# Two fp16 parts instead of three bf16 parts, and attention scores of two heads side by side in TensorE

## Chip, cores and metric

The kernel runs on one core of one Trainium2 chip. The metric is the device time of a run in microseconds, the median of several runs. Engines: PE (TensorE, matmuls), ACT (ScalarE), DVE (VectorE), POOL (GpSimd), SP (SyncE, which here only issues DMAs).

## The reference

One block of a gated cross-attention layer and one of a self-attention layer with a mixture of experts. Cut to what matters (`B, L, D = 4, 512, 256`, 16 heads of 16):

```
q = layernorm(x) @ wq.T + bq;  k, v = ctx @ wk.T + bk, ctx @ wv.T + bv
x = x + tanh(g_xattn) * (softmax(q k^T / 4) v)              # per batch and head, 512 x 512 scores
s = layernorm(x);  q, k = rope(s @ Wq), rope(s @ Wk_c @ Wk);  v = s @ Wv_c @ Wv
y = rmsnorm(s + (softmax(q k^T / 4) v) @ Wo)
x = x + tanh(g_ffn) * rmsnorm(y + shared_ffn(y) + top2_experts(y))
```

Everything is fp32 in the reference.

## The kernel before

The attention is done in eight instances `INST`: four cross (one for each batch), then four self. An instance has four groups of four heads (`NG`, `HG`), a group has 16 steps (`STEPS`), one for each unit: one head and one tile of 128 keys against 512 queries. So there are 512 units in 32 groups.

- **Parts.** q and k are split into three bf16 parts each (`NPART`), whose products of six terms (`NTERM`, `Q_PART`, `K_PART`) give the precision of fp32. The terms stand one above the other in 96 rows (`STK`). Part one is a copy by ACT (`first_part`, `part0`), `rest` a subtraction on POOL, part two a copy by ACT (`second_part`, `part1`), part three a subtraction on POOL (`third_part`, `part2`). SP writes the parts to DRAM and loads them back stacked, four DMAs for each group (`stack`).
- **Maxima.** `max_pair` makes the scores of one head with queries on the partitions, two tiles of queries into two banks, and DVE's `row_max` reduces both (L1136). Banks 2 to 5 are a ring of two such pairs. Eight maxima make a group; they run `LEAD` = 12 maxima ahead of the exps. DVE splits the 16 maxima of a group into two bf16 parts (`m2`), PE turns them (`turn_max`, after step `AT_MAX` = 9), ACT copies them to `mTs` and, at step `AT_ROWS` = 11, issues the DMA that puts them as two more rows (98, `KROWS`) below the stack of q. They stand against ones in k, so that the score matmul subtracts the maximum.
- **Units.** PE makes the scores of a unit (L1653) with keys on the partitions, ACT the exp into `prob` (L891, `scale=SC`), and after every fourth unit PE multiplies four heads with their values (`values`, L1629; fp32, each head with its 17 output rows in its own 32 columns of the array). `copy_values` copies a group's sum to `oT`, `turn_heads` turns it (L1617, in the ring), and DVE's `heads_out` divides.
- **Three banks.** Scores, turned maxima and all tiles of the projections of later instances take turns in `SCORE_BANKS` = 0, 1, 7; `take` waits until the slot three places back is empty.
- **Hooks.** `CROSS_STEPS`, `SELF_STEPS` and `FA_STEPS` say at which step relative to an instance the work for the next one (statistics, norm, tiles, parts) and for the output of the last is put into each engine's order. The engines run their orders strictly; the steps are written out by hand. A cross instance has ten tiles, a self instance nine, an output four. A tile is made by PE and emptied by ACT or DVE (`OWNER`).
- **After** the last group follow the feed-forward part, sorting and experts (from 538 us on), which the change leaves alone. SP's order is `stack(n)` for one instance after another.

Of the kernel before, what the change touches and what calls it, by code (L numbers as in the profile page):

```python
# [7 lines left out]
BF16 = mybir.dt.bfloat16  # L8
# [26 lines left out]
def flamingo_block(nc, x, ctx_in, g_xattn, g_ffn, wq, bq, wk, bk, wv, bv,  # L35
# [27 lines left out]
    SCR = [16 * 5, 16 * 3]  # L63
    SC = 1.0 / float(DH) ** 0.5
    VM = DH + 1
    MROWS = MPART * HG * TT
# [13 lines left out]


    HOOKS = {}

    def hook(n, step, *what):
# [3 lines left out]
    CROSS_STEPS = [("stats", 0, -34), ("norm", 1, -20), ("norm", 0, -16), ("tile", 2, -12), ("empty", 2, -12), ("tile", 0, -11),  # L88
        ("empty", 0, -11), ("tile", 3, -10), ("empty", 3, -10), ("tile", 1, -6), ("empty", 1, -6), ("tile", 4, -5),
        ("empty", 4, -5), ("tile", 5, -5), ("empty", 5, -5), ("tile", 6, -4), ("empty", 6, -4), ("part0", 0, -3),  # L90
        ("part1", 0, 1), ("rest", 0, 1), ("empty", 8, 2), ("tile", 8, 2), ("part2", 0, 2), ("tile", 7, 3),
        ("empty", 7, 3), ("part0", 1, 3), ("rest", 1, 4), ("tile", 9, 5), ("empty", 9, 5), ("part1", 1, 7),
        ("part2", 1, 10)]
    SELF_STEPS = [("stats", 0, -28), ("norm", 0, -21), ("norm", 1, -20), ("tile", 0, -14), ("empty", 0, -14), ("tile", 1, -9),
        ("empty", 1, -8), ("tile", 4, -4), ("empty", 2, -3), ("empty", 4, -3), ("tile", 2, -3), ("tile", 3, -2),
        ("empty", 3, -2), ("tile", 5, -1), ("empty", 5, 0), ("sum", 0, 1), ("tile", 6, 2), ("empty", 6, 2),
        ("sum", 1, 2), ("tile", 7, 5), ("empty", 7, 5), ("part0", 0, 5), ("rest", 0, 5), ("tile", 8, 7),
        ("empty", 8, 7), ("rest", 1, 8), ("part2", 1, 8), ("part0", 1, 10), ("part1", 0, 14), ("part2", 0, 14),
        ("part1", 1, 16)]
    FA_STEPS = [("fatile", 0, 12), ("faempty", 0, 12), ("faempty", 1, 15), ("fatile", 1, 15), ("faempty", 2, 19), ("fatile", 2, 19),  # L100
        ("fatile", 3, 23), ("faempty", 3, 23), ("fastats", 0, 32), ("nf", 0, 43)]

    SELF_NO = {m: sum(k_ == "s" for k_, _ in INST[:m + 1]) for m in range(NI)}
    for n in range(1, NI):
        m = n + 1
        if m < NI:
            for what, i, step in (CROSS_STEPS if INST[m][0] == "c" else SELF_STEPS):
                hook(n, step, what, m, i)
        if INST[n - 1][0] == "s":
            for what, i, step in FA_STEPS:  # L110
                hook(n, step, what, INST[n - 1][1], i)

# [12 lines left out]
    for u_ in range(NI * UNITS):  # L125
        n_, g_, s_ = u_ // UNITS, u_ // STEPS % NG, u_ % STEPS
        SLOTS.append(("unit", u_))
# [94 lines left out]
    with es:  # L222
# [23 lines left out]
        identb = sb("identb", [P, P], BF16)  # L246
# [26 lines left out]
        pp = mix[:, 0:NPART * 2 * L].bitcast(BF16).rearrange("p (x r o l) -> p x r o l", x=2, r=NPART, o=2)  # L273
# [6 lines left out]
        stacks = w2[:].rearrange("p k e d -> p (k e d)").bitcast(BF16).rearrange("p (x g h l) -> p x g h l", x=2, g=NG, h=HG)  # L280
        qs = stacks[0:KROWS, 0]
        ks = stacks[0:KROWS, 1]
        oT = sb("oT", [P, L], F32)
        negm = sb("negm", [P, 2, HG, TT], F32)

        m2 = sb("m2", [P, 2, P], BF16)
        mTs = sb("mTs", [MROWS, 2, P], BF16)
# [50 lines left out]

        scrq = nc.dram_tensor("scrq", [2, NTERM, DH * NH, L], BF16, kind="Internal").ap()
        scrk = nc.dram_tensor("scrk", [2, NPART, DH * NH, L], BF16, kind="Internal").ap()  # L340
# [22 lines left out]
        s_r0 = [sem(f"first_rest_ready{i}") for i in range(2)]  # L363
        s_p1 = [sem(f"second_part_ready{i}") for i in range(2)]
# [95 lines left out]
        def _(sp):  # L460
# [39 lines left out]
            def next_ctx(b):  # L500

                sp.wait_ge(s_ta, EMPTIED["proj", INST.index(("c", 0 if b == 2 else b - 1)), 3][1])
                load_ctx(b, ctxs[:])

            def stack(n):
                par = n % 2

                for g in range(NG):
                    ge(sp, s_stk[g], (n - 1) * 64)

                def put(X, part, ready):
                    sp.wait_ge(ready[X], n + 1)
                    p_ = parts[X][:, part]
                    if X or Q_PART.count(part) == 1:
                        d_ = (scrk[par, part] if X else scrq[par, Q_PART.index(part)]).rearrange("(o p) t -> p o t", p=P)
                        sp.dma_start(d_, p_).then_inc(s_scr[X], 16)
                        return
                    r = Q_PART.index(part)
                    c = Q_PART.count(part)
                    for o in range(2):  # L520
# [1320 lines left out]
```

## Time and profile before

| | us |
|---|---|
| median of 3 runs (789.3 to 790.07) | 789.88 |
| profiled run | 793.59 |
| its span | 791.8 |

| engine | busy us | share |
|---|---|---|
| PE | 746.5 | 94% |
| DVE | 512.4 | 65% |
| ACT | 408.1 | 52% |
| PE's weight loads | 342.7 | 43% |
| POOL | 225.6 | 28% |

Busy time is the union of an engine's instructions. Matmuls overlap in their pipeline: one alone takes some 0.38 us from start to end, but two that follow each other are shown as x2 with 0.60 us. So what counts is from start to start. In the timeline and the chain, a bracket at the end of a line gives the idle time before it and what ended it.

### The profile page before, as it was taken

To read this page: it belongs to the slowest core of one execution; us is meant where nothing else is said; L and a number is where in the kernel's file an instruction comes from. 1 tells how busy PE (TensorE), PEld (TensorE's weight loads), DVE (VectorE), ACT (ScalarE), POOL (GpSimd) and SP (SyncE) were. 2 spreads that over 40 slices of the span, in tenths; PEclk is the share of its full clock that TensorE was granted. 3 is DMA by queue.
4 is the path that set the end of the run, shared out by engine and by line. 5 is a ranking of instruction groups with operands and counts; after the bars stand their busy time and mean duration, and the time that the engine had idled before them with its cause. 6 is when DMAs were issued, how large, how long until landed. Compare 5 with 4: busy or idle time off the path is not lost.

```text
span 791.8 us, 10350 instructions
## 1 busy us (share of the span) xinstructions
PE 746.5 (94%) x3510; PEld 342.7 (43%) x3510; DVE 512.4 (65%) x777; ACT 408.1 (52%) x766; POOL 225.6 (28%) x342
## 2 busy tenths in 40 slices
PE   5889999999999999999999999999999999989994
PEld 3432343243233233233323423425645755458883
DVE  2588847956978878878797798743366022623764
ACT  2437867777767767876675777683211122222000
POOL 3360222314315405304222410010105622400654
PEclk9989999999999999999999999999999999999997
DMA  7792334216215414513411341006003734000010
GB/s 233 207 256 57 81 84 144 79 32 204 63 50 164 122 41 126 141 41 94 146 43 40 125 112 47 1 2 213 0 0 125 272 115 133 0 1 1 34 41 34
DMA packets 51892, 73.31 MB, mean 93 GB/s; under 512 B 7808, under 2 KB 42880, under 8 KB 51840
## 3 DMA queue, kind: packets, MB, share of 16 engines
q1 hardware_dynamic: 47248, 63.80, 27.4%
q0 software_dynamic: 2816, 8.46, 2.8%
q10 hardware_dynamic: 1776, 0.40, 0.3%
q8 instruction: 29, 0.48, 0.3%
q14 instruction: 23, 0.19, 0.1%
HBM read 45.04 MB, written 27.33 MB: 91 GB/s over the span
## 4 chain that ended last, share of the span: by engine, by line
PE 75%; DVE 14%; ACT 5%; issue 3%; DMA 1%; POOL 1%; ACTq 0%; DVEq 0%; POOLq 0%
PE ps L1483 35%; PE ps L1629 12%; PE ps L1653 11%; PE ps L1603 10%; DVE negm L1136 7%; ACT hS L891 3%; PE ps L1478 2%; DVE bst L1014 2%; PE ps L1617 1%; PE ps L1542 1%; DMA bv_bc<-in_L_xattn_bv_dram 1%; PE ps L1537 1%; PE ps L1563 0%; POOL out_dram L753 0%; DVE rows L1021 0%
## 5 line engine op out<-in xcount | busy, mean ns | idle before, releaser
L1136 DVE TENSOR_REDUCE negm<-ps 128x2 f32<-128x1024 f32 x256 | 304.0, 1221 | 75.8 <-PE ps L1603 68.0
L891 ACT ACTIVATE hS<-ps 128x512 f32<-128x512 f32 x512 | 280.6, 604 | 116.2 <-PE ps L1653 114.4
L1653 PE MATMUL ps<-w 98*128 98x512 bf16 x512 | 170.6, 386 | 4.8 <-DVE qk L1069 1.9
L1603 PE MATMUL ps<-w 96*128 96x512 bf16 x512 | 154.9, 383 | 7.3 <-DVE negm L1136 6.4
L1629 PE MATMUL ps<-hS,mix 128*17 128x512 f32 x1024 | 134.7, 598 | 0.2
L1653 PEld LDWEIGHTS ps<-w 98*128 98x128 bf16 x512 | 44.0, 97 | 157.0 <-ACT hS L891 76.7
L1603 PEld LDWEIGHTS ps<-w 96*128 96x128 bf16 x512 | 47.9, 99 | 59.7 <-DVE negm L1136 13.2
L1335 DVE SCALAR_TENSOR_TENSOR ctxs<-qk,ps 128x512 f32<-128x512 f32 x32 | 22.0, 688 | 76.3 <-ACT qk L925 51.1
L925 ACT ACTIVATE qk<-ps 128x512 f32<-128x512 f32 x32 | 19.1, 597 | 82.5 <-PE ps L1483 78.6
L1483 PE MATMUL ps<-w,hS 128*128 x256 | 55.7, 379 | 2.0 <-issue 2.0
L1483 PEld LDWEIGHTS ps<-w,hS 128*128 128x128 f32 x256 | 48.6, 190 | 9.4 <-issue 2.9
L615 POOL TENSOR_TENSOR mdif<-bst 128x4 f32<-128x4 f32 x12 | 2.5, 206 | 156.5 <-DVEq L976 156.5
L653 POOL TENSOR_SCALAR hS<-hS,tg 128x256 f32<-128x256 f32 x16 | 14.9, 931 | 99.6 <-DVEq L1162 99.6
L638 POOL TENSOR_TENSOR qk<-qk,mix 128x1024 f32<-128x1024 f32 x14 | 29.8, 2130 | 42.9 <-ACT mix L811 42.6
L633 POOL TENSOR_TENSOR qk<-qk,hT 128x1024 f32<-128x1024 f32 x8 | 18.8, 2350 | 76.1 <-DVEq L976 76.1
L1629 PEld LDWEIGHTS ps<-hS,mix 128*17 128x17 f32 x1024 | 17.0, 95 | 53.9 <-ACT hS L891 29.9
L643 POOL TENSOR_TENSOR mix<-qk,mix 128x1024 bf16<-128x1024 f32 x14 | 29.9, 2133 | 22.6 <-ACT mix L815 21.6
L1483 PE MATMUL ps<-fout,hS 128*128 128x256 f32 x128 | 30.6, 396 | 1.8 <-issue 1.8
L1483 PE MATMUL ps<-cT,fin 128*128 128x512 f32 x64 | 28.6, 595 | 0.7 <-ACT cT L918 0.7
L725 POOL DMA_INDIRECT scrf<-rows,place x16 | 15.7, 980 | 47.0 <-DVEq L976 42.4
L1338 DVE SCALAR_TENSOR_TENSOR hS<-ctxs,ps 128x512 f32<-128x512 f32 x32 | 22.0, 687 | 10.3 <-PE ps L1483 8.8
L1483 PEld LDWEIGHTS ps<-fout,hS 128*128 128x128 f32 x128 | 25.3, 199 | 7.3 <-issue 3.8
(210 smaller groups left out, 875.5 us busy)
## 6 DMA issues: line engine op xcount, KB each, us to landing
w<-scrq SPq DMA_DIRECT2D x32, 384.0 KB, 4.5
scrk<-mix SPq DMA_DIRECT2D x24, 256.0 KB, 2.1
scrq<-mix SPq DMA_DIRECT2D x16, 384.0 KB, 3.3
scrq<-mix SPq DMA_DIRECT2D x24, 256.0 KB, 2.5
w<-scrk SPq DMA_DIRECT2D x32, 192.0 KB, 2.9
w<-scrk SPq DMA_DIRECT2D x32, 128.0 KB, 2.9
w<-in_L_ffn_W_experts_dram SPq DMA_DIRECT2D x8, 512.0 KB, 8.0
mix<-scrf SPq DMA_DIRECT2D x4, 528.0 KB, 5.5
```

The costliest lines, as they stand in the source:

```text
L633: link(pool.tensor_tensor(qk[X][:], qk[X][:], rb[X], ALU.add))
L638: link(pool.tensor_tensor(qk[X][:], qk[X][:], parts[X][:, 0], ALU.subtract))
L643: link(pool.tensor_tensor(parts[X][:, 2], qk[X][:], parts[X][:, 1], ALU.subtract))
L891: nc.scalar.activation(prob[:, kt % PROB_SLOTS, s % HG, :], slot_bank(("unit", u)), ACT.Exp, scale=SC).then_inc(s_exp, 1)
L925: nc.scalar.activation(th[k % 4], end_full(f"{name}{b}", 2 * p), ACT.Tanh, scale=0.5).then_inc(s_th, 1)
L1136: V.tensor_reduce(negm[:, gi % 2, h, 2 * t2:2 * t2 + 2], ps[:, bank:bank + 2, :], AX.X, ALU.max, negate=True).then_inc(s_re, 1)
L1335: V.scalar_tensor_tensor(out=uu[:, k % 2, :], in0=th[k % 4], scalar=1.0, in1=end_full(f"{name}{b}", 2 * p), op0=ALU.add, op1=ALU.mult).the ...
L1338: V.scalar_tensor_tensor(out=hS[:, b * TT:(b + 1) * TT, p, :], in0=uu[:, k % 2, :].rearrange("p (t j) -> p t j", t=TT), scalar=0.5, in1=en ...
L1483: last = MM(o, w, r, start=(j == 0), stop=(j == len(terms) - 1))
L1603: last = MM(ps[:, bank + t, :], qs[0:STK, g, h, tt * P:(tt + 1) * P], ks[0:STK, g, h, :], start=True, stop=True)
L1629: last = MM(ps[32 * h:32 * h + VM, 6, :], vp[n % 2][:, kt, g * HG + h, :], prob[:, kk % PROB_SLOTS, h, :], start=(kt == 0), stop=(kt == TT ...
L1653: MM(take(("unit", u)), ks[:, g, h, kt * P:(kt + 1) * P], qs[:, g, h, :], start=True, stop=True).then_inc(s_sT, 1)
```

## The change

- q and k are first multiplied by a power of two ("fit") so that two fp16 parts hold them; the products need three terms, so a stack has 48 rows, and 50 with the two rows of the maxima (now divided by 32768, against 32768 in k).
- The powers come from the largest magnitude of contexts, weights and biases: DVE reduces them per partition (`magnitudes`), ACT's queue stores and reloads them across partitions, DVE computes powers, scaled biases and the scale of the exp (`powers`). Four such events: two at the start, two in the loop. The first part of k in the first instance waits for the first of them. The exp takes its scale from a tensor (`scale=esc[:, e:e+1]`).
- `second_part` and `third_part` are gone. What was `rest` now gives the second part.
- Stacks of two heads stand side by side in partitions 0 to 63 and 64 to 127 (`qs[j]`, `ks[j]`). `max_pair` takes one tile of queries of two heads instead of two tiles of one head. The scores come two units at once into two of the three banks, at even steps.
- `LEAD` 12 becomes 16, `AT_MAX` 9 becomes 11, `AT_ROWS` 11 becomes 15; the DMAs of the maximum rows (now two) go from ACT's queue to SP's, and SP's order follows the steps too (`put`, `get`, `max_rows`). All hook tables have other steps.
- ACT no longer waits for all biases before its first copy, and the value bias has a semaphore of its own. A tanh at the start loads ACT's table early.

```diff
-NTERM = 6
-NPART = 3
-Q_PART = [0, 0, 0, 1, 1, 2]
-K_PART = [0, 1, 2, 0, 1, 0]
-LEAD = 12
+NTERM = 3
+NPART = 2
+Q_PART = [0, 0, 1]
+K_PART = [0, 1, 0]
+HALF = 64
+MAX_ONE = 32768.0
+LEAD = 16
+PUT_LAG = 3
-AT_COPY, AT_HEADS, AT_MAX, AT_ROWS = 4, 8, 9, 11
+AT_COPY, AT_HEADS, AT_MAX, AT_ROWS = 3, 8, 11, 15
...
+    CROSS_STEPS = [("stats", 0, -38), ("mags", 0, -36), ("put", 0, -32), ("get", 0, -30), ("powers", 0, -26),
+        ("norm", 1, -20), ("norm", 0, -16), ("tile", 0, -11), ("empty", 0, -11), ("tile", 2, -11), ("empty", 2, -11),
+        ("tile", 3, -9), ("empty", 3, -9), ("tile", 1, -6), ("empty", 1, -6), ("tile", 4, -5), ("empty", 4, -5),
+        ("tile", 6, -3), ("empty", 6, -3), ("tile", 5, -1), ("empty", 5, -1), ("part0", 0, -1), ("empty", 8, 2),
+        ("tile", 8, 2), ("tile", 7, 3), ("empty", 7, 3), ("rest", 0, 4), ("tile", 9, 5), ("empty", 9, 5),
+        ("part0", 1, 5), ("rest", 1, 6)]
+    SELF_STEPS = [("stats", 0, -28), ("norm", 0, -22), ("norm", 1, -18), ("tile", 0, -15), ("empty", 0, -15),
+        ("tile", 1, -8), ("empty", 1, -7), ("tile", 4, -4), ("empty", 4, -3), ("empty", 2, -2), ("tile", 2, -2),
+        ("tile", 5, 0), ("empty", 5, 0), ("tile", 3, 1), ("empty", 3, 2), ("sum", 0, 3), ("empty", 6, 5), ("tile", 6, 5),
+        ("sum", 1, 6), ("part0", 0, 7), ("rest", 0, 7), ("empty", 7, 8), ("tile", 7, 8), ("tile", 8, 9), ("empty", 8, 9),
+        ("part0", 1, 14), ("rest", 1, 18)]
...
+        qs = [stacks[HALF * j:HALF * j + KROWS, 0] for j in range(2)]
+        ks = [stacks[HALF * j:HALF * j + KROWS, 1] for j in range(2)]
...
+            def max_rows(gi):
+                sp.wait_ge(s_mts, gi + 1)
+                n_ = MPART * HP * TT
+                for j in range(2):
+                    sp.dma_start(qs[j][STK:KROWS, gi % NG, :, :], mTs[j * n_:(j + 1) * n_, gi % 2, :]).then_inc(s_mrow, 16)
...
+            def put_magnitudes(e):
+                c, n_ = EVENTS[e]
+                act.wait_ge(s_mag, e + 1)
+                act.dma_start(scra[e], am[:, c:c + n_], allow_slow_non_contiguous=True).then_inc(s_mst, 16)
+
+            def get_magnitudes(e):
+                n_ = EVENTS[e][1]
+                act.wait_ge(s_mst, 16 * (e + 1))
+                ge(act, s_fit, e)
+                act.dma_start(amall[:, 0:P * n_], scra[e].rearrange("p n -> (p n)").unsqueeze(0).to_broadcast([P, P * n_])).then_inc(s_mld, 16)
...
                         nc.scalar.activation(prob[:, kt % PROB_SLOTS, s % HG, :], slot_bank(("unit", u)),
-                                             ACT.Exp, scale=SC).then_inc(s_exp, 1)
+                                             ACT.Exp, scale=esc[:, e:e + 1]).then_inc(s_exp, 1)
...
-                h, t2 = p // 2, p % 2
+                hp, tt = divmod(p, TT)
...
-                for t in range(2):
-                    tt = 2 * t2 + t
-                    last = MM(ps[:, bank + t, :], qs[0:STK, g, h, tt * P:(tt + 1) * P], ks[0:STK, g, h, :],
+                for j in range(2):
+                    last = MM(ps[:, bank + j, :], qs[j][0:STK, g, hp, tt * P:(tt + 1) * P], ks[j][0:STK, g, hp, :],
                               start=True, stop=True)
...
-                            pe.wait_ge(s_mrow, (gi + 1) * 16)
-                        MM(take(("unit", u)), ks[:, g, h, kt * P:(kt + 1) * P], qs[:, g, h, :],
-                           start=True, stop=True).then_inc(s_sT, 1)
+                            pe.wait_ge(s_mrow, (gi + 1) * 16 * 2)
+                        if s % 2 == 0:
+                            banks = [take(("unit", u + j)) for j in range(2)]
+                            for j in range(2):
+                                MM(banks[j], ks[j][:, g, h // 2, kt * P:(kt + 1) * P], qs[j][:, g, h // 2, :],
+                                   start=True, stop=True).then_inc(s_sT, 1)
```

## Rows read from the trace of the kernel before

**Rows 1.** Stretches: stretch, length, busy us of each engine, PE's clock, DMA.

```profile
114.10:176.90 62.80, 61.42 (x326) 22.14 (x325) 44.92 (x57) 46.57 (x89) 17.93 (x23) 1.00 0.33 98
239.80:300.60 60.80, 59.47 (x308) 19.28 (x308) 50.06 (x61) 44.64 (x85) 22.63 (x24) 1.00 0.37 108
```

**Rows 2.** Timeline of PE, one quad: start, length, engine, line, tiles, count.

```profile
215.87 0.61 PE L1653 MATMUL ps<-w 98*128 98x512 bf16 x2
216.31 0.60 PE L1603 MATMUL ps<-w 96*128 96x512 bf16 x2
...
217.71 1.05 PE L1629 MATMUL ps<-hS,mix 128*17 128x512 f32 x8
218.69 0.60 PE L1653 MATMUL ps<-w 98*128 98x512 bf16 x2
```

**Rows 3.** Timeline at the loop's end, where there are no maxima.

```profile
523.49 0.82 PE L1653 MATMUL ps<-w 98*128 98x512 bf16 x3
523.92 2.06 ACT L891 ACTIVATE hS<-ps 128x512 f32<-128x512 f32 x4 [0.68 <-PE ps L1653]
...
524.57 0.39 PE L1653 MATMUL ps<-w 98*128 98x512 bf16 x1 [0.26 <-ACT hS L891]
...
525.88 0.82 PE L1653 MATMUL ps<-w 98*128 98x512 bf16 x3
...
537.51 0.66 PE L1617 MATMUL ps<-identf,oT 128*128 128x128 f32 x4 [0.72 <-ACT oT L779]
```

**Rows 4.** Timeline of PE at a turn of heads.

```profile
260.52 0.60 PE L1617 MATMUL ps<-identf,oT 128*128 128x128 f32 x4
260.95 0.38 PE L1653 MATMUL ps<-w 98*128 98x512 bf16 x1
```

**Rows 5.** Timeline of DVE, maxima without a wait between them.

```profile
516.52 3.49 DVE L1136 TENSOR_REDUCE negm<-ps 128x2 f32<-128x1024 f32 x3
```

**Rows 6.** Timeline of PE at a full tile and at one with 64 rows.

```profile
233.73 1.88 PE L1483 MATMUL ps<-nT,fq 128*128 128x512 f32 x4
235.45 0.38 PE L1653 MATMUL ps<-w 98*128 98x512 bf16 x1
...
239.76 0.39 PE L1653 MATMUL ps<-w 98*128 98x512 bf16 x1 [0.49 <-DVE qk L1069]
240.08 1.12 PE L1537 MATMUL ps<-cT,fkv 64*128 64x512 f32 x2
241.13 0.39 PE L1653 MATMUL ps<-w 98*128 98x512 bf16 x1
```

**Rows 7.** Groups of ACT's instructions: count, busy us, mean ns, idle before.

```profile
L891 ACT ACTIVATE hS<-ps 128x512 f32<-128x512 f32 x512 | 280.6, 604 | 116.2 <-PE ps L1653 114.4
L779 ACT ACTIVATE oT<-ps 128x512 f32<-128x512 f32 x32 | 19.2, 600 | 1.2 <-PE ps L1629 1.2
...
L815 ACT ACTIVATE mix<-qk 128x1024 bf16<-128x1024 f32 x14 | 14.9, 1065 | 1.6 <-POOLq L639 0.8 <-ACT mTs L784 0.8
...
L825 ACT ACTIVATE qk<-ps,bqk 128x512 f32<-128x512 f32 x12 | 8.2, 687 | 19.4 <-PE ps L1483 17.0 <-PE ps L1563 2.5
```

**Rows 8.** Timeline of the start: first part, maximum, maximum rows, first score.

```profile
16.32 0.69 ACT L846 ACTIVATE mix<-ps,bqk 128x512 bf16<-128x512 f32 x1 [1.92 <-PE ps L1483]
...
37.89 1.23 DVE L1136 TENSOR_REDUCE negm<-ps 128x2 f32<-128x1024 f32 x1 [7.54 <-PE ps L1603]
...
50.11 0.73 ACTq L789 DMA_DIRECT2D w<-mTs  x1
...
52.44 0.37 SPq L516 DMA_DIRECT2D scrk<-mix  x1
...
52.53 0.61 PE L1603 MATMUL ps<-w 96*128 96x512 bf16 x1 [2.38 <-DVE negm L1136]
...
54.49 1.06 PE L1653 MATMUL ps<-w 98*128 98x512 bf16 x2
```

**Rows 9.** The chain that ended last, in order: start, length, what.

```profile
4.05 7.28 DMA bv_bc<-in_L_xattn_bv_dram
```

More of the change, by code:

```diff
@@ L94, in flamingo_block @@
[L94 to L99, printed above, removed]
@@ L106, in flamingo_block @@
         if m < NI:
+            last = 0
             for what, i, step in (CROSS_STEPS if INST[m][0] == "c" else SELF_STEPS):
                 hook(n, step, what, m, i)
+                if what in ("part0", "rest"):
+                    hook(n, step + PUT_LAG, "put_first" if what == "part0" else "put_rest", m, i)
+                    last = max(last, step + PUT_LAG)
+            STACK_AT[m] = last + 1
         if INST[n - 1][0] == "s":
@@ L111, in flamingo_block @@
                 hook(n, step, what, INST[n - 1][1], i)
+    for n in range(NI - 1):
+        for g in range(NG):
+            hook(n, max((g + 1) * STEPS, STACK_AT[n + 1]) + 1, "stack", n + 1, g)
+    hook(1, 4, "next", 3, 0)
+    for i in range(N_LATE):
+        hook(i + 1, 6, "late", 0, i)
     BEGIN = [2, 3, 6, 7, 0, 1, 4, 5, 8, 9]
@@ new lines, in put @@
+                    ge(sp, s_stk[g], (n - 1) * STACKED)
+                sp.wait_ge(s_spl[X] if part else s_p0[X], n + 1)
+                p_ = parts[X][:, part]
+                scr, terms = (scrk, K_PART) if X else (scrq, Q_PART)
+                at = [r for r in range(NTERM) if terms[r] == part]
+                if len(at) == 1:
+                    sp.dma_start(scr[n % 2, at[0]].rearrange("(o p) t -> p o t", p=P), p_).then_inc(s_scr[X], 16)
+                    return
+                r0, dr = at[0], at[1] - at[0]
@@ L558, in _ @@
             assert len(late) == N_LATE
-            stack(0)
+            sp.wait_ge(s_one, 1)
+            for X in (1, 0):
+                for part in range(NPART):
+                    put(0, X, part)
+            for g in range(NG):
+                get(0, 1, g)
+                get(0, 0, g)
             next_ctx(2)
@@ L824, in cross_tile @@
                         ge(act, s_spl[X], m)
-                    nc.scalar.activation(qk[X][:, o, :], full(key), ACT.Identity, bias=bqk[:, X, o:o + 1]).then_inc(s_ta, 1)
+                    act.wait_ge(s_fit, AT_EVENT[INST[m]] + 1)
+                    b = INST[m][1]
+                    f = 1 + b if X else 0
+                    nc.scalar.activation(qk[X][:, o, :], full(key), ACT.Identity, bias=bfit[:, f, o:o + 1],
+                                         scale=fit[:, f:f + 1]).then_inc(s_ta, 1)
             def self_tile(m, t):
@@ L1106, in empty @@
+                ready(s_spl[X])
             def empty(m, t):
@@ L1196, in _ @@
                                 stats(m)
+                            elif what == "mags":
+                                magnitudes(AT_EVENT[INST[m]])
+                            elif what == "powers":
+                                powers(AT_EVENT[INST[m]])
                             elif what == "empty" and OWNER[INST[m][0]][i] == "V":
@@ L1608, in turn_max @@
                 pe.wait_ge(s_m2, gi + 1)
-                o = take(("turned", gi))[:, 0:P // 2].bitcast(BF16)
-                last = TR(o, m2[:, gi % 2, :], identb[:])
+                o = take(("turned", gi))[:, 0:P // 2].bitcast(F16)
+                last = TR(o, m2[:, gi % 2, :], identh[:])
                 last.then_inc(s_mtf, 1)
```

345 lines of the change are left out of this document (187 added, 158 removed).

## The prediction

> **What bounds the kernel now.** The page first: PE is busy 94% of the span, DVE 65%, ACT 52%. I then read the groups by line, for what repeats, and the stretches, for one period of the attention loop (64 units of scores) for either kind of instance. In both stretches PE is at 98%, DVE at 72 to 82%, ACT at 73 to 74% [rows 1]. The last view is PE's timeline, because a busy PE may still be waiting inside its pipeline. There the loop is a fixed pattern, which I call a quad: four score matmuls, four maximum matmuls, four value products. There [rows 2] give 218.69-215.87 = 2.82 us per quad: eight matmuls at 0.2175 (two from 215.87 to 216.31; 1.74), 0.98 for the value products (217.71 to 218.69), and 0.10 left for the step into them. So PE's stream is the bound, in the stages 54.49 to 537.5 (483 us; first score and last turn of heads, [rows 3, 8]). The other 309 us aren't touched but for the start. A period sums to its work plus stalls: 122 quads at 2.82 and 6 at 2.39 (without maxima, [rows 3]) are 358; turned heads 32 x 0.44 [rows 4]; turned maxima 32 x 0.10; tiles 1.72 for a product (235.45-233.73, [rows 6]), about 0.44 for a transpose (as for heads), 1.05 for a small one (241.13-240.08): ten tiles of a cross instance 12.1, nine of a self instance 10.2, four of an output 4.3, together 78. Sum 453. So 30 of the 483 us are stalls.
>
> **The score and maximum matmuls.** Two heads with 50 (or 48) rows each go to partitions 0 and 64 and to two banks. If both stream at once, a pair takes 0.22 instead of 0.435. No row shows matmuls side by side in the rows of the array. The nearest are the value products: four heads in four column groups, fp32, x8 records in 1.05 [rows 2], where one after the other would be 8 x 0.2175 = 1.74; so side by side works there in full. Bounds 0.22 and 0.435; I take 0.22, being nearest to that row. PE's own work per quad falls to 4 x 0.2175 + 1.08 = 1.95, 0.87 less; that is 122 x 0.87 = 106 us if nothing else were late.
> The Trainium skill (TensorE: Matmul & The Clock Gate, section on packing small matmuls) says that row groups overlap too, with starts some 4 ns apart; by it the same 0.22 stands. No row here shows it.
>
> **What is late next: the exchange with ACT.** Before, a unit takes the next of three banks, so a score waits for the exp three units back. Now a pair takes two of three, and waits until the first exp of the pair before it is done. The tail without maxima shows the links: score start to exp start 0.43 (523.49 to 523.92), exp end to next score 0.05 (524.52 to 524.57) [rows 3]. The exp gets its scale from a tensor instead of a constant. The nearest row is the Identity with a bias from a tensor, 687 ns against 600 for the copy of the same size and 604 for the exp [rows 7]: bounds 0.60 and 0.69, I take 0.69, as that row has the operand. x4 in 2.06 gives 0.487 from exp to exp now, so 0.575 then, still under PE's pace.
> From the first pair of a quad to the second: 0.43+0.69+0.05 = 1.17, PE working 0.44 of it. From the second pair to the next quad: pair and maxima 0.44, step 0.10, values 0.98 = 1.52. A quad is 2.69, not 1.95: a gain of 0.13, with 0.73 of idle PE in the first half where a small piece can hide. At 0.60 per exp it would be 2.60. In the tail 1.17+1.30 = 2.47. All: 120 x 2.69 + 8 x 2.47 = 343, 15 less than 358.
> The Trainium skill (ScalarE: Activation LUTs, section on what an ACTIVATE and a table load cost) gives 93 ns for each pointer operand; the trace's 87 agrees, and by 93 the quad is 0.01 longer. It is the rule that speaks against this change.
>
> **Drains.** A 64-row product between full ones starts 0.32 after a matmul that needs 0.22, and ends after 1.05 where 0.86 would do: 0.30 for in and out [rows 6]. A full tile among full ones pays none: its 1.72 are four times 0.43. After the change the scores are 64-row and all full tiles pay 0.30; the 64-row tiles of k and v save it. Turned heads (0.44+0.30) mostly hide in the idle half: 0.4 each, 13 in all. Turned maxima 0.25: 8. A tile also takes a slot of the three banks, so the pair behind it waits for both exps (1.17 becomes 1.74). By the hooks: cross tiles 12.4 x 2, self tiles 8.9 x 4 (three of them in the idle half), outputs 4.3 x 3: 73. Together 94 against 95 before: nothing gained.
>
> **ACT.** The second parts (two copies of 1.065 per instance, [rows 7]) go; they were off the path. But ACT now has only 2.69-2.31 = 0.38 to spare in a quad. A norm (two at 0.49) costs 0.6 twice, a first part (1.05) about 0.8 once: 2 us for each of six instances, 12. Copies to oT 32 x 0.1 = 3. The maximum rows move to SP and to step 15, behind its puts and gets. Issue to landing was 2.3 (50.11 to 52.44, [rows 8]); from the turn at step 11 to the next group are 0.25+1.17+1.52 = 2.9, the chain needs about 3.1: 0.2 x 31 = 6. Exp, score and value product of the next group are behind that wait. SP's stacks are loaded 9 or more units before use, and carry half the bytes: zero, worth up to 1 us a stage if the cover went.
>
> **DVE.** A maximum is 1.221 long and 1.14 apart (3.49 for x3, [rows 5]): 2.27 in a quad of 2.69. Its lumps (statistics, rotations, heads) catch PE through the two-slot ring. I take 1.5 per instance, 9, and 3 for magnitudes and powers of two instances (for each a reduction of 1024 elements like a maximum, 1.2, and some 14 tiny ones with their waits; estimate 3.5, half of it in DVE's spare time; at most 4 each). The smaller splits on POOL are off the path.
>
> **The loop after:** 343+94+12+3+6+12 = 470, against 483: -13.
>
> **The start.** LEAD 16 instead of 12 puts four more maxima ahead of the first exp: 4 x 1.14 = +4.6. The magnitudes add reduction, store, load and powers before the first part of k, which began at 16.32 [rows 8]. A load landed after 7.28 there [rows 9]; I take 4 each way. Against that, ACT no longer waits for the value bias before copying cT, the third part is gone, and the stacks have half the bytes. First maximum 37.89 before, 37 to 44 after, I take 38.5: +0.6. POOL's memset lies beside the loads. Net +5.2.
>
> **Sum.** -13+5 = -8. The profiled run took 793.59 (span 791.80, 1.8 around it), the runs have the median 789.88, 3.7 under it. So 785.6 for a profiled one, and 789.9-8 = 782 as the median.
>
> **Rivals.**
> 1. The lumps overlap better than I add them, since each engine has 10 to 20% to spare. PE's load is 128 x 1.95+94 = 344, so the time is set by DVE (358 in the loop now, less overlap, some 366 after) and the exchange. If the drains hide too and stalls are 30 as now, the loop is 343+78+30 = 451: 789.9-32+5 = 763. For it: the idle 0.73 in every quad. Against it: one pair of lookahead. Chance 0.25.
> 2. Slower: a pair of banks leaves ACT no cushion, so its lumps go straight to PE. They are 11 to 12.6 per instance (8 copies at 0.49, norms 2.0, parts 2.1, oT 2.0, maxima 0.7). I count 12 of some 72 us; if half count, the loop is 494 and the time 789.9+11+5 = 806. It decides from 20 of the 72 on (then the loop has saved less than the start costs). For it: quads are at 2.69 with ACT at 2.31. Chance 0.3.
> 3. The pairs don't run side by side: the second half of a quad is 0.44 longer, 128 x 0.44 = 56: 838. Against it the value products. Chance 0.05.
> 4. The clock: with less work PE may be granted less. At 54.49 two matmuls took 1.06 instead of 0.61, after a wait of 2.38 on DVE in the lead [rows 8, 2]. With 16 maxima of 0.22 in 1.14 that lasts longer; a quad then costs 1.7 more, for 4 us of loop 2 to 3. In the range.
>
> **Chances.** Forecast (770 to 794) 0.4, rival 1 0.25, rival 2 0.3, rival 3 0.05. 0.2% (1.6 us) is about what a measurement can tell from no change. Of the forecast's 0.4, 0.24 lies under 788.3, 0.09 within, 0.07 above. Faster 0.5, same 0.1, slower 0.4 with the others. The range takes 754 to 810; the forecast's own is 770 to 794.
>
> **What would show it.** Right: PE's timeline with a pair in 0.22 and about 1.17 from the first to the second pair of a quad; the exp at 0.69; PE busy 85% in the loop, waits of the score load on the exp in most units. Wrong: quads under 2.5 (exchange mis-sized), first exp later than 61 or earlier than 56, waits on the maximum rows or stacks over 1 us per group, pairs at 0.43.

## The result and the profile after

The changed kernel takes 828.95 us (median of 4 runs, 824.61 to 833.34); the kernel before took 789.59 beside it. The ratio is 1.050, 95% interval 1.043 to 1.058: slower by 39 us, where 782 was forecast. Profiled were a run of 832.15 after and one of 793.59 before.

The page after: busy time, and PE and its granted clock in 40 slices of 20.8 us.

```profile
span 830.4 us, 10656 instructions
...
PE 690.9 (83%) x3510; PEld 302.5 (36%) x3510; DVE 523.8 (63%) x827; ACT 449.7 (54%) x753; POOL 192.3 (23%) x327
...
PE   5586788858878978878887888887999999999994
...
PEclk9795989989999999999999997998999999999998
```

The stretch from the first score to the last turn of heads, first the one of before, then the one of after (columns as in [rows 1]).

```profile
54.49:537.51 483.02, 469.76 (x2476) 160.11 (x2474) 374.07 (x471) 348.10 (x665) 125.67 (x212) 1.00 0.30 88
```

```profile
71.33:579.41 508.08, 411.74 (x2470) 120.98 (x2466) 373.24 (x493) 390.51 (x653) 96.54 (x145) 0.94 0.16 50
```

PE's busy time in the loop fell from 469.8 to 411.7, yet the loop took 25.1 more, and in it the granted clock fell from a mean of 1.00 to one of 0.94. There are two levels, 1.0 (2.4 GHz) and 0.5 (1.2 GHz), so that is 0.06/0.5 x 508 = 61 us at the lower one. The first score came 16.8 later. What follows the loop took 251.0 in place of 254.3.

The timeline of two quads after, PE and ACT (answering [rows 2, 3]).

```profile
84.39 0.39 PE L1753 MATMUL ps<-w 50*128 50x512 f16 x2 [0.65 <-ACT hS L943]
84.61 0.40 PE L1701 MATMUL ps<-w 48*128 48x512 f16 x2
84.93 1.05 PE L1727 MATMUL ps<-hS,mix 128*17 128x512 f32 x8
85.92 0.39 PE L1753 MATMUL ps<-w 50*128 50x512 f16 x2
86.14 0.38 PE L1701 MATMUL ps<-w 48*128 48x512 f16 x2
86.34 2.51 ACT L943 ACTIVATE hS<-ps,esc 128x512 f32<-128x512 f32 x4 [0.27 <-PE ps L1753]
87.17 0.39 PE L1753 MATMUL ps<-w 50*128 50x512 f16 x2 [0.65 <-ACT hS L943]
```

A pair is 0.39 long and the next matmul starts 0.22 after it: the two run side by side. From the first pair of a quad to the second are 87.17-85.92 = 1.25, from the second to the next quad 85.92-84.39 = 1.53: a quad of 2.78, against 2.82 before. PE stands 0.65 in it for the exp.

This is the shortest form. The next quad has the copy to `oT` ahead of its exps:

```profile
88.70 0.39 PE L1753 MATMUL ps<-w 50*128 50x512 f16 x2
88.83 0.60 ACT L819 ACTIVATE oT<-ps 128x512 f32<-128x512 f32 x1
...
90.15 0.39 PE L1753 MATMUL ps<-w 50*128 50x512 f16 x2 [0.85 <-ACT hS L943]
...
91.68 0.39 PE L1753 MATMUL ps<-w 50*128 50x512 f16 x2
```

PE stands 0.85 and the quad takes 2.98. Over all quads at the full clock that hold nothing but their four scores, four maxima and value products (counted by the starts of the matmuls in the two traces), before has 54 with a median of 2.82 and a mean of 2.91, after has 47 with 2.98 and 3.03. So the quads, which were to become 0.13 shorter, became longer on average.

The start (answering [rows 8, 9]): the chain of waits, and the timeline of ACT and DVE.

```profile
9.51 5.95 DMA scra<-am
15.49 4.20 DMA w<-scra
...
32.88 8.52 DMA scra<-am
41.42 5.05 DMA w<-scra
...
170.76 7.56 DMA scra<-am
178.34 4.59 DMA w<-scra
```

```profile
22.71 1.45 ACT L894 ACTIVATE mix<-ps,bfit,fit 128x512 f16<-128x512 f32 x2 [5.75 <-DVEq L1028]
...
41.80 0.60 ACT L864 ACTIVATE cT<-ps 128x512 f32<-128x512 f32 x1 [4.43 <-DMA scra<-am]
...
46.50 0.29 DVE L1095 TENSOR_REDUCE amx<-w 128x1 f32<-128x128 f32 x1 [9.42 <-DMA w<-scra]
...
49.91 1.23 DVE L1230 TENSOR_REDUCE negm<-ps 128x2 f32<-128x1024 f32 x1 [1.99 <-PE ps L1701]
```

The first part of k came at 22.71 in place of 16.32, and the first maximum at 49.91 in place of 37.89: the second event's load stands in DVE's order ahead of the maxima. The second of the two events inside the loop, on ACT and PE:

```profile
178.72 0.69 ACT L943 ACTIVATE hS<-ps,esc 128x512 f32<-128x512 f32 x1 [5.79 <-DMA scra<-am]
...
180.62 0.61 PE L1753 MATMUL ps<-w 50*128 50x512 f16 x2 [5.78 <-ACT hS L943]
...
181.58 1.91 PE L1727 MATMUL ps<-hS,mix 128*17 128x512 f32 x8
```

ACT's next exp stands behind the wait for its own store, PE behind ACT, and afterwards the value products take 1.91 where they take 1.05 at the full clock. The first event in the loop (store at 99.78) goes another way: its store landed after 1.4 and its load after 3.1, and there PE stood for a maximum, because DVE's search for magnitudes stood ahead of it:

```profile
101.22 0.61 PE L1701 MATMUL ps<-w 48*128 48x512 f16 x2 [2.00 <-DVE negm L1230]
```

From 100 us on the clock is at the lower level for some 10 us there too.

### The profile page after: what moved, and what is told of

It is laid out like the page before. It is cut to its first block, busy times and chain, and to the rows that moved or that the text cites. A ratio compares the mean times of both kernels' runs of the same rounds, so it can differ in the third digit from the quotient of the medians.

```text
span 830.4 us, 10656 instructions
## 1 busy us (share of the span) xinstructions
PE 690.9 (83%) x3510; PEld 302.5 (36%) x3510; DVE 523.8 (63%) x827; ACT 449.7 (54%) x753; POOL 192.3 (23%) x327
## 4 chain that ended last, share of the span: by engine, by line
PE 51%; DVE 17%; ACT 15%; issue 7%; DMA 6%; POOL 2%; ACTq 0%; DVEq 0%; POOLq 0%
PE ps L1582 30%; ACT hS L943 11%; DVE negm L1230 9%; PE ps L1727 8%; PE ps L1753 6%; PE ps L1701 3%; DMA scra<-am 3%; POOL scrf L762 2%; PE ps L1715 2%; DMA w<-scra 2%; PE ps L1577 1%; DVE bst L1133 1%; ACT rows L845 1%; DVE qk L1177 1%; DMA bqk<-in_L_xattn_bq_dram 1%
## 5 line engine op out<-in xcount | busy, mean ns | idle before, releaser
L943 ACT ACTIVATE hS<-ps,esc 128x512 f32<-128x512 f32 x512 | 323.4, 684 | 85.4 <-PE ps L1753 77.2
L1753 PE MATMUL ps<-w 50*128 50x512 f16 x512 | 105.1, 402 | 76.6 <-ACT hS L943 67.7
L1727 PE MATMUL ps<-hS,mix 128*17 128x512 f32 x1024 | 144.9, 640 | 0.4 <-ACT hS L943 0.4
L1701 PE MATMUL ps<-w 48*128 48x512 f16 x512 | 108.4, 403 | 18.2 <-DVE negm L1230 15.6
L1753 PEld LDWEIGHTS ps<-w 50*128 50x128 f16 x512 | 28.5, 93 | 215.6 <-ACT hS L943 125.4
L685 POOL TENSOR_TENSOR mix<-qk,mix 128x1024 f16<-128x1024 f32 x14 | 30.0, 2142 | 76.6 <-ACT mix L859 75.9
L1701 PEld LDWEIGHTS ps<-w 48*128 48x128 f16 x512 | 27.0, 95 | 52.1 <-DVE negm L1230 22.6
L1250 DVE RECIPROCAL rec<-ps 128x16 f32<-128x16 f32 x32 | 8.1, 254 | 35.8 <-PE ps L1715 35.8
L1582 PE MATMUL ps<-rope_sb,fin 128*128 128x512 f32 x64 | 28.2, 593 | 0.0
L1582 PE MATMUL ps<-wT,fin 128*128 128x512 f32 x64 | 28.1, 592 | 0.0
```

What stands on the lines that cost most here:

```text
L685: link(pool.tensor_tensor(parts[X][:, 1], qk[X][:], parts[X][:, 0], ALU.subtract))
L943: nc.scalar.activation(prob[:, kt % PROB_SLOTS, s % HG, :], slot_bank(("unit", u)), ACT.Exp, scale=esc[:, e:e + 1]).then_inc(s_exp, 1)
L1582: last = MM(o, w, r, start=(j == 0), stop=(j == len(terms) - 1))
L1701: last = MM(ps[:, bank + j, :], qs[j][0:STK, g, hp, tt * P:(tt + 1) * P], ks[j][0:STK, g, hp, :], start=True, stop=True)
L1727: last = MM(ps[32 * h:32 * h + VM, 6, :], vp[n % 2][:, kt, g * HG + h, :], prob[:, kk % PROB_SLOTS, h, :], start=(kt == 0), stop=(kt == TT ...
L1753: MM(banks[j], ks[j][:, g, h // 2, kt * P:(kt + 1) * P], qs[j][:, g, h // 2, :], start=True, stop=True).then_inc(s_sT, 1)
```

## The experiments

Where nothing else is said a time is a median, and the kernel before took 788.5 to 789.3 beside each set of runs. "Profiled" is the time of the run whose trace was kept. "Start" is the time of its first score, "loop" the stretch from there to its last turn of heads. The profiled run can lie some us to either side of the median, so starts and loops are compared with that in mind. Ratios are to the kernel before.

| kernel | us | ratio, 95% interval | profiled | start | loop | clock in span |
|---|---|---|---|---|---|---|
| before | 789.6 |  | 793.6 | 54.49 | 483.0 | 0.986 |
| after | 828.95 | 1.043 to 1.058 | 832.2 | 71.33 | 508.1 | 0.949 |
| e1_const | 794.72 | 1.004 to 1.010 | 799.0 | 50.97 | 494.0 | 0.962 |
| e2_const_single | 798.04 | 1.007 to 1.013 | 799.0 | 52.60 | 492.3 | 0.968 |
| e3_const_serial | 910.16 | 1.134 to 1.155 | 911.3 | 54.00 | 603.1 | 0.876 |
| e4_late_get | 813.83 | 1.029 to 1.035 | 813.6 | 70.19 | 491.0 | 0.962 |
| e5_const_imm | 783.18 | 0.991 to 0.996 | 779.2 | 51.21 | 473.8 | 0.981 |
| e6_const_early | 810.31 | 1.026 to 1.031 | 807.8 | 51.30 | 502.1 | 0.958 |
| e7_const_warm | 798.74 | 1.010 to 1.017 | 799.3 | 56.26 | 490.5 | 0.973 |
| e8_pe_mags | 812.40 | 1.026 to 1.033 | 814.3 | 56.35 | 501.9 | 0.959 |
| e9_before_ptr | 801.45 | 1.013 to 1.020 | 797.9 | 50.52 | 495.0 | 0.991 |
| e10_pe_mags2 | 810.36 | 1.024 to 1.033 | 806.4 | 53.98 | 496.4 | 0.966 |
| e11_const_imm_lead12 | 777.53 | 0.981 to 0.989 | 780.5 | 47.21 | 480.8 | 0.970 |
| e12_const_imm_single | 780.07 | 0.985 to 0.992 | 780.2 | 52.09 | 475.6 | 0.981 |
| e13_before_short | 862.66 |  | 869.1 | 55.99 | 558.8 | 0.902 |
| e14_own_mags | 799.49 | 1.011 to 1.020 | 798.6 | 53.34 | 493.0 | 0.972 |
| e15_pe_mags2_lead12 | 802.99 | 1.009 to 1.019 | 804.3 | 50.21 | 498.2 | 0.971 |

**The whole search for magnitudes taken out** (e1). Constant powers of two stand in `fit`, `bfit` and `esc`; the scale of the exp is still a tensor.

```diff
-        ("mags", 0, -36), ("put", 0, -32), ("get", 0, -30), ("powers", 0, -26),
+            for f, v in enumerate(FITS):
+                mark(V.memset(fit[:, f:f + 1], v))
```

> The changed kernel without the search for magnitudes: the powers of two, the scaled biases and the scale of the exp are constants set at the start, so no reductions of magnitudes, no store and reload across partitions, no waits for them; everything else stays, the exp still reads its scale from a tensor. Theory A (the four magnitude events, with the waits of ACT and DVE in order and the lower clock behind them, carry most of the loss): the first score comes at about 57 instead of 71.3 us, the groups around 100 and 175 us lose their 5 and 10 us, and the time is 829-31 = 798. Rival B (the exchange of score banks with ACT carries it): the events cost no more than the 5 us forecast for them, and the time stays at 818 or more.

Measured 794.72, 34 under after. The search was costed at 3 + 0.6 us in the sum; it is the larger part of the loss, 20 us of it ahead of the first score (71.33-50.97) and 14 in the loop.

**Only the reload later** (e4). It is the changed kernel with `("get", 0, -22)` and `("powers", 0, -14)` in place of -30 and -26.

> The changed kernel with the reload of the magnitudes moved from 2 to 10 steps behind their store in ACT's order (and the powers from step -26 to -14); only for the two events in the loop. Theory A: ACT no longer stands 5.8 us and 1.4 us before the reload, and PE's clock does not fall there: 10 to 14 us less, about 817. Rival: what ACT waited for was hidden by PE, and the time is within 3 us of 829.

Measured 813.83, 15 less, all of it in the loop (508.1 to 491.0). So the loop's share of the loss comes with where store, reload and powers stand in the orders, and the search's own work is not needed to explain it.

**What of the search costs** (e14, e8, e10, e15). In e14 every instruction of the search stays and only the way across the partitions is left out:

```diff
-                dve.wait_ge(s_mld, 16 * (e + 1))
-                link(V.tensor_reduce(amx[:, c:c + n_], amall[...], AX.X, ALU.max))
+                for i in range(c, c + n_):
+                    mark(V.memset(amx[:, i:i + 1], LARGEST[i]))
```

> The changed kernel with its search and the arithmetic of the powers on DVE at their steps, but the largest magnitudes set to fixed values in place of the store, the load and the reduction across partitions, which it leaves out. Theory A, the crossing costs the most: e1_const (795) plus DVE's own 3 to 6 us: 797 to 802. Rival B, DVE's instructions in the order of the maxima cost most of it: 806 to 812.

Measured 799.49: the search's own work costs 799.5-794.7 = 5 (an uncertain figure, since e1's ten runs spread from 789.9 to 800.3), the crossing 829.0-799.5 = 29. The first maximum stands at 31.89 there, 18.0 before the 49.91 of after, and the first score also 18.0 before (53.34 against 71.33): the start's loss is the crossing, one for one.

e8 crosses by a matmul, `MM(bank, am[:, c:c + 1].to_broadcast([P, P]), identf)`, whose 128 columns hold the values of all partitions on every partition; no DMA is left.

> The changed kernel with its search for magnitudes whole, but each column of magnitudes brought to all partitions by one matmul against the identity in a bank of the scores, in place of the store to DRAM and the load back. Theory A, the events cost by their two transfers and by the engines that stand behind them: e1_const (795) plus the search's own work on DVE (3 to 5 us): 798 to 801, first score near 57 us. Rival B, the search's instructions and its order on DVE cost most of it: 810 or more.

Measured 812.40, as rival B had it. The start is 15 better than after's, but the loop only 6, where e14's is 15 better. PE's timeline tells why:

```profile
87.66 2.05 PE L1570 MATMUL ps<-identf,am 128*128 128x128 f32 x8 [4.45 <-DVEq L1012]
...
89.75 0.69 DVE L1080 TENSOR_REDUCE amx<-ps 128x4 f32<-128x512 f32 x1 [2.29 <-PE ps L1570]
...
90.18 1.91 PE L1729 MATMUL ps<-hS,mix 128*17 128x512 f32 x8
```

I had put PE's matmul at the same step as DVE's search. PE stood 4.45 for DVE, then DVE 2.29 for PE, and the clock fell: again engines that stand in order for each other. e10 sets search, matmul and arithmetic apart by 5 steps and one.

> e8_pe_mags (812) with the steps of an event apart: the search of the weights at step -41, that of the context at -38, the matmuls at -33 and the arithmetic at -32, so that PE and DVE no longer stand for each other (PE stood 4.45 us for the search, DVE 2.29 for the matmuls, and the clock fell behind them). Theory A, an event costs by the engine that stands in order for another: 802 to 806, group 3 of 19.7 us going to 14 to 15. Rival B, by its own instructions on DVE (4.5 us in event 2), which keep the maxima's banks from PE wherever they stand: 809 to 813.

Measured 810.36 (806.39 to 812.78), inside rival B's range, so setting the steps apart bought 2 us at most. The profiled run, the fastest of the four, has its loop 5.5 shorter than e8's. What the median still loses against e1 was not taken apart further: it can be DVE's own instructions, as the rival says, or the clock, which in the two slower runs is 0.953 and 0.954 and in the fastest 0.966. e15 is that kernel with `LEAD` 12, and computes all that the changed kernel does.

> e10_pe_mags2 (810, profiled span 804.6) with twelve pairs ahead of the loop in place of sixteen; nothing of the computation is left out. Theory A, -5 as e11_const_imm_lead12 against e5_const_imm: 801 to 806, still over before. Rival B, DVE's search and not the lead sets the first score: 808 to 812.

Measured 802.99, within the expected range: 26 better than the changed kernel, 14 worse than the one before.

**The exp's scale as an immediate** (e5, e9). e5 is e1 with `scale=SC / (...)`, a number.

> Leaves the search for magnitudes out (constant powers of two, as in e1_const) and gives the exponential its scale as an immediate again. In e1_const three exps in a row take 1.93 us (0.58 each beyond the first), before 1.57 (0.49), and PE stands 0.65 us in each quad for them. Theory A, the exchange of two banks for two exps sets the quad now: one pair of each quad waits, two exps less 0.087 each, so -0.17 x 128 = -22 from e1_const's 795: 773 (768 to 782), quads of 2.85 going to 2.68. Rival B, the quad is set by the matmuls and their drains and the wait is only shifted: 790 to 795, ACT idle grows by what the exps give back.

Measured 783.18, 11.5 less than e1. It is Theory A's side, but half its size: 22 were expected, and 783.2 is outside its 768 to 782. The shortest of its quads:

```profile
203.44 0.39 PE L1756 MATMUL ps<-w 50*128 50x512 f16 x2
...
203.87 2.23 ACT L939 ACTIVATE hS<-ps 128x512 f32<-128x512 f32 x4 [0.63 <-PE ps L1756]
204.60 0.39 PE L1756 MATMUL ps<-w 50*128 50x512 f16 x2 [0.56 <-ACT hS L939]
...
206.13 0.39 PE L1756 MATMUL ps<-w 50*128 50x512 f16 x2
```

From first pair to second it is now 1.16, to the next quad 1.53: 2.69, against 2.78. One exp of each quad lies in the chain, not two: 0.09 x 128 = 11.5. Some of the difference of the medians is the clock's: e1's three runs with a clock of 0.977 took 789.9 to 791.9, e5's three with 0.974 and 0.975 took 782.4 to 784.2, some 8 apart. The other way round, the kernel before with a scale from a tile:

> The kernel before, its exponential given the same scale from a tile in place of an immediate. Theory A, the 0.09 us that each exp takes longer is hidden where PE sets the quad (2.82 us, against four exps in a row of 4 x 0.58 = 2.31): 789 to 792. Rival B, it costs wherever it stands, as e1_const against e5_const_imm (12 us): 799 to 803.

Measured 801.45, so the rival was right and PE's cover did not exist. The clock is no part of it (0.991 in the span, 0.986 before). A quad of the kernel before, with the load of the fourth score's weights (PEld):

```profile
128.12 0.60 PE L1653 MATMUL ps<-w 98*128 98x512 bf16 x2
...
128.55 2.06 ACT L891 ACTIVATE hS<-ps 128x512 f32<-128x512 f32 x4 [1.02 <-PE ps L1653]
...
129.00 0.59 PE L1653 MATMUL ps<-w 98*128 98x512 bf16 x2
129.19 0.10 PEld L1653 LDWEIGHTS ps<-w 98*128 98x128 bf16 x1 [0.32 <-ACT hS L891]
```

The same place in e9, and the starts of the next two quads:

```profile
128.95 0.61 PE L1658 MATMUL ps<-w 98*128 98x512 bf16 x2
...
129.38 2.42 ACT L895 ACTIVATE hS<-ps,esc 128x512 f32<-128x512 f32 x4 [0.49 <-PE ps L1658]
...
129.83 0.68 PE L1658 MATMUL ps<-w 98*128 98x512 bf16 x2
...
130.12 0.10 PEld L1658 LDWEIGHTS ps<-w 98*128 98x128 bf16 x1 [0.41 <-ACT hS L895]
...
131.86 0.60 PE L1658 MATMUL ps<-w 98*128 98x512 bf16 x2
...
134.77 0.39 PE L1658 MATMUL ps<-w 98*128 98x512 bf16 x1
```

Quads of 2.91 in place of 2.82: again 0.09 x 128 = 11.5, and the loop grew by 12.0. So two ways lead from a quad's first score to its fourth. On PE it is five matmuls: 5 x 0.2175 = 1.09. Through ACT the fourth score needs the bank of the first: 0.43 to its exp, 0.60 for the exp, 0.04 to the load of the weights (129.19-128.55-0.60), and some 0.03 to the matmul, 1.10 in all. In the kernel before the two ended together, beside a PE that was busy throughout. With the longer exp the load comes at 130.12-128.95 = 1.17 in place of 129.19-128.12 = 1.07, and the two last scores show 0.68 in place of 0.59: the fourth waits. So this link was a second bound of the same length from the start, and pairs that stream in half the time could shorten only what stands behind it. In the changed kernel that part fell from 1.73 to 1.53, and the link itself grew from 1.10 to 1.25.

**Scores side by side** (e2, e12, e3). e2 and e12 give each unit its own step and bank again:

```diff
-                            banks = [take(("unit", u + j)) for j in range(2)]
-                            for j in range(2):
-                                MM(banks[j], ...)
+                        MM(take(("unit", u)), ks[h % 2][...], qs[h % 2][...], ...)
```

> As the kernel without magnitudes, and in addition each unit takes its own bank and is multiplied at its own step again, as before the change; two heads still stand one above the other, maxima are still made in pairs. This undoes only that a pair of scores takes two of three banks. If the exchange with ACT sets the quad (2.78 us in the changed kernel), a score now waits for the exp three units back and a quad falls to about 2.45 (PE: six slots of 0.2175, 0.10, 0.98 = 2.39; ACT 4 x 0.575 = 2.31): 0.3 x 128 = 38 us less than the kernel without magnitudes, some 5 to 10 of it given back by DVE, about 768. If PE's drains and the tiles set it, the time is that of the kernel without magnitudes or 128 x 0.2 more, since the scores no longer run side by side.

> e5_const_imm (783) with the scores' matmuls one bank and one step each again (each still 50 rows high, the maxima still side by side); leaves the search for magnitudes out. Theory A, with the immediate PE sets the quad, and each single score pays its own streaming and drain as in the kernel before: quads from 2.68 back to 2.8, 128 x 0.13 = +17 at most, 790 to 797. Rival B, ACT and the exchange set it, as e1_const and e2_const_single were alike: 781 to 786.

Measured 798.04 against e1's 794.72 and 780.07 against e5's 783.18. The first is 30 over the 768 of its main case and in the range of its other one (no change, or up to 26 more); the second is 1 under the rival's range. The differences have opposite signs and are about as large as the spread of the runs. Taking two banks at a time for the scores of two heads is worth 3 us at most in either direction. In e3 both matmuls of a pair use the same 64 rows, so that they must follow each other; the odd heads of its output come from the even heads' stacks.

> As the kernel without magnitudes, but both matmuls of every pair, scores and maxima, read the stacks of partitions 0 to 63, so both stand in the same rows of the array and can't run side by side; the scores of the odd heads are therefore those of their neighbours. The order of the instructions and all waits are the same. If side by side works as the timeline shows (two in 0.39), the second half of each quad is 0.44 longer, 128 x 0.44 = 56 us more than the kernel without magnitudes; if PE has that much to spare behind ACT and DVE, under 20.

Measured 910.16 (896.07 to 912.06), 115 over e1, and 101 in its fastest run. As expected, the pairs do run side by side in e1; the size is twice the 56. Groups of e3 at the full clock take 13.46 where those of e1 take 11.9 to 12.1 (the time between two turned maxima): 1.4 x 32 = 45 for the streaming. The other 70 go with the clock: groups of 22.8 stand there with the clock at 0.50, and from 100 to 140 us PE is busy 40.00 of 40.00 at that level. This was the first sign of what e13 tells below.

**The maximum rows earlier** (e6): `AT_MAX, AT_ROWS = 5, 8` in place of 11, 15, as sixteen pairs of lead allow.

> Leaves the search for magnitudes out, as e1_const; the turned maxima are taken at step 5 of a group in place of 11 and their rows loaded at step 8 in place of 15. Theory A: the rows of maxima end their load after the scores of the next group are due (14 waits of about 1 us, 13.5 us in the profile of after): these go, -8 to -13 from 795: 782 to 787. Rival B: the waits hid the exchange with ACT, which is late next: 792 to 796.

Measured 810.31, 16 worse where 8 to 13 better were expected. By the turns of heads the profiled loop is 8.1 longer: nothing in the self instances (a period of 60.0 for 60.2), 2.1 in one group of the cross instances, 2.3 in the last two full groups, the rest in small. So in the self instances the rows' load was no bound. The move also puts other work of ACT and SP at other steps, so in the cross instances it can't be told from that. Why it is slower, and what the median has beyond the profiled loop, stays open.

**PE kept busy ahead of the loop** (e7): 144 small matmuls in the lead.

> Leaves the search for magnitudes out, as e1_const, and adds 16 + 16 x 8 small fp16 matmuls on PE between the maxima ahead of the loop, into a bank not yet in use, so that PE does not stand idle there. Theory A, the fall of the clock ahead of the loop costs 5 to 8 us (granted clock 0.5 from 43 to 68 us in e1_const, group 1 of 20.4 us): clock stays at 1.0 over 45 to 68 us, the group falls to about 14 to 16, 787 to 790 in all. Rival B, DVE's maxima and the row load set that stretch at either clock: 794 to 797.

Measured 798.74, 4 worse. The clock held to 1.00 in most of the lead, the first score came 5.3 later, and the clock fell at 60 us all the same. It bought nothing; but since the added matmuls also put off the first score, it does not tell what a lead at the full clock alone would give.

**The lead** (e11): `LEAD` 12 in e5.

> e5_const_imm (783) with twelve pairs of maxima ahead of the loop in place of sixteen; leaves the search for magnitudes out. Theory A, each of the four maxima stands ahead of the first score with 1.15 us: -4.6, 778 to 779. Rival B, another wait ends last there (the rows' load, the parts of the second instance): 782 to 784.

Measured 777.53, -5.7 (-4.6 expected), with the start 4.0 earlier. It leaves the search out, so it is no substitute for either kernel.

**What the clock follows** (e13). The kernel before, its matmuls of maxima and scores 48 rows high:

```diff
-                    last = MM(ps[:, bank + t, :], qs[0:STK, g, h, ...], ks[0:STK, g, h, :],
+                    last = MM(ps[:, bank + t, :], qs[0:48, g, h, ...], ks[0:48, g, h, :],
-                        MM(take(("unit", u)), ks[:, g, h, ...], qs[:, g, h, :],
+                        MM(take(("unit", u)), ks[0:48, g, h, ...], qs[0:48, g, h, :],
```

> The kernel before with the matmuls of maxima and scores 48 rows high in place of 96 and 98, the same columns and order; leaves out the three smaller of the six products of parts and the maxima's two rows. Theory A, low matmuls let the granted clock fall, busy PE or not (e3_const_serial: over 200 us at 0.50 with 94% busy): falls inside the loop, clock under 0.975, 797 to 830. Rival B, the falls follow PE's waits: clock as before (0.986), 787 to 791.

The products left out are the last three terms; by `Q_PART` and `K_PART` one of them (q's second part with k's first) is no smaller than one that stays, which changes nothing in the timing. Measured 862.66, above both ranges: 73 us longer (before: 789.33 beside it) with half the rows in these matmuls, and still 52 longer in the fastest run. Stretches of before, then of e13, on PE alone (start and end, length, PE busy, clock, DMA):

```profile
80.00:100.00 20.00, 18.96 (x113) 1.00 0.29 77
100.00:150.00 50.00, 48.91 (x256) 1.00 0.36 106
```

```profile
80.00:100.00 20.00, 20.00 (x64) 0.50 0.14 34
100.00:150.00 50.00, 50.00 (x166) 0.62 0.08 23
150.00:200.00 50.00, 49.11 (x262) 1.00 0.40 118
```

The same instructions in the same order were granted 1.00 in every such stretch of before. Both kernels enter the loop at the lower level, after PE stood 2.3 us for a maximum in the lead; before is back at the full clock within 5 us, e13, with PE never standing, stays at the lower level from 60 to 135 us. Later it falls again, with PE busy 98.55 of 100 us from 200 to 300 (clock 0.88; before 97.82 at 1.00). The loop's mean is 0.86. The four runs say the same: 841.17, 856.21, 869.12 and 869.82 us at mean clocks of 0.938, 0.916, 0.902 and 0.900.

What this does in the changed kernel is not shown. In e13 and e3 some 50 rows work at a time; in after, e1 and e5 two stacks of 50 do, side by side, and e5's loop has a mean clock of 0.99. And the falls in after come where PE had been standing: the one at 178.8 us within the wait of 5.78, the one near 510 us after this:

```profile
505.00:510.00 5.00, 3.26 (x25) 0.99 0.18 52
```

So for after PE's waits are the cause at hand. That is argued; no run tells the two apart there.

The Trainium skill (TensorE: Matmul & The Clock Gate, section on why this matters for your kernels) asks for a busy TensorE without idle gaps. e13 was busy for all of 80 to 100 us at 0.50, so here that was not enough; the measurement decides.

## Why the prediction was wrong

The forecast was 782, the time 829: 47 to explain. The experiments add up to the time: 783 with an immediate scale and no search (e5), the tensor scale +11.5 (e1), the search's instructions +5 (e14), the crossing +29 (after). The forecast had the same terms: 3+0.6 for the search, 120 x 0.087 = 10.4 for the tensor scale, so 768 for what e5 is. Of the 47, then, 30 are the search (34 in place of 3.6), 15 the rest of the change (783 in place of 768), 1 the scale.

**The start, +16.8 for +5.2.** LEAD's four maxima were right (4.6 forecast; 4.8 is what the stretch from first maximum to first score grew, and 4.0 the start between e5 and e11). The step that failed is "+0.6" for the first maximum: it counts one event, "before the first part of k". The second one, for the second context, stands in DVE's order just ahead of the first maximum (9.42 of idle). "I take 4 each way" was short too: the ways took 5.95 and 4.20, and in the second event 8.52 and 5.05; but the first part of k came only 6.4 later. The first maximum was forecast for 38.5, within 37 to 44, and came at 49.91, 12.0 later than before. Without the crossings it came at 31.89 (e14), so all else in the start was faster than I took it to be. "First exp later than 61" was named as a sign of being wrong, and it came.

**The search in the loop.** It was costed as 3 us on DVE, with nothing for the queue. The instruction that starts the reload waits on ACT for the store (7.56), and the next exp is queued behind it: 5.79 of idle on ACT, 5.78 on PE, in the second event of the loop. This was in the diff; I did not ask what stands behind a DMA's wait on the engine that issues it. With the wait moved (e4) the loop is as short as without any search (491.0 and 494.0).

**Side by side.** Right: 0.22 for a pair, as forecast; the third rival did not happen. The working that led there had a slip: 8 x 0.2175 = 1.74 is the pace of the bf16 matmuls, while an fp32 record takes 0.43 (1.72 for the four of a full tile, [rows 6]). One after the other the value products would take 8 x 0.43 = 3.44, so 0.98 shows side by side even more clearly; the conclusion stands.

**The quad.** 2.69 forecast, 2.78 measured at best, and for an immediate 2.60 and 2.69. The mechanism was right (first to second pair by way of ACT, then PE's 1.52) and one link was short: exp end to next score was taken as 0.05 from [rows 3]; here it is 87.17-86.34-0.68 = 0.15, in e5 204.60-203.87-0.60 = 0.13. What makes the difference was not tried. About 0.09 x 120 = 11 us. The copies to oT were taken at 0.1 for each of 32 groups; where a quad holds nothing else the copy costs 0.20 (2.98 in place of 2.78), so by an estimate from that row 6 us in place of 3. These 14 are most of e5's 15.

**PE as the only bound.** "PE's stream is the bound" was half of the truth: e9 shows that from first to fourth score a second way of the same length lies beside it. I had its links in [rows 3] and used them for after, but never for before, where 0.43+0.60+0.05 = 1.08 against PE's 5 x 0.2175 = 1.09 would have shown it.

**The clock.** Rival 4 gave it 2 to 3 us, only at the start. In the loop it was at the lower level for some 60 us after, 40 in e1 (0.04/0.5 x 494), and before only in the first 5 us. What a fall costs: the group of turned maxima that ends near 522 in after takes 16.57, the same one in e4 at the full clock 13.07. The two stretches:

```profile
510.00:520.00 10.00, 9.12 (x42) 0.50 0.05 16
```

```profile
500.00:510.00 10.00, 8.22 (x61) 1.00 0.14 41
```

So 3.5 us for about 10 at the lower level, and for 61 an estimate of 20 us. It is part of the crossing's 29 and of e1's distance to the forecast, not on top of them. That the clock would fall inside the loop, where waits of PE now stand, is what no step of mine had; whether the lower matmuls add to it (e13) stays open for this kernel.

**Rivals.** The second (806) had the right side and the right place in ACT, but by lumps of copies; these did cost in the instances with cross tiles (groups of 25.0 to 26.4 in e1 where before had 23.9) and not in the self instances (a period of 60.2 for 60.9). Drains and maximum rows were not measured one by one. e1's loop is 494 against 467 forecast without the search; the quad's link explains 11 of the 27, the copies to oT 3 and the clock's 40 us some 13, the last two by estimates. That the rest cancels can be luck.

## What to carry to other kernels

Where an engine is busy 98% of the time, ask in the kernel before what every other way between the same two instructions would take. Here it was 1.10 us against 1.09: faster matmuls gave nothing on that stretch, and 0.09 us more on the other way cost 12 us at once. A wait for a DMA belongs on an engine with nothing queued behind it; the same bytes cost 15 us less when only the steps between store, reload and powers grew. Work taken out of TensorE can be paid for in its clock, by the waits that appear (after) or by rows that are no longer used (e13), so read the granted clock of the loop before and after.

## What the runs showed of the hardware that was not expected

- TensorE, 97% busy in the loop with matmuls 96 and 98 rows high, was granted 1.00 in it but for the first 5 us; with the same matmuls 48 rows high it stood at the lower level for about 156 of 559 us (0.14/0.5), 98% busy, and the kernel was 73 us slower in the median.
- Two matmuls of 50 rows at partitions 0 and 64 into two banks run side by side: a pair starts the next work 0.22 after it, as one alone.
- A store of 0.5 to 2.5 KB and the load that brings it back to all partitions took 5.95 and 4.20, 8.52 and 5.05, 7.56 and 4.59, so 10 to 14 us there and back in three of the four events; the fourth (2.0 KB, at 99.78 us) took 1.4 and 3.1. What makes it so much faster was not looked into.
- An exp of 512 elements takes 604 ns with an immediate scale and 684 with a tensor's; an Identity with scale and bias from tensors 777 (L872 in after), where one tensor operand made 687 [rows 7].
